# Attention values with v stationary in four column tiles, normalised once a sequence, and the turn loop written out

## The chip, the cores and the metric

The kernel runs on one NeuronCore of a Trainium2 chip. The metric is the device time of one launch in microseconds (us). Engine names: TensorE (PE; PEld is its weight loads), VectorE (DVE), ScalarE (ACT), GpSimd (POOL), SyncE (SP, which only issues transfers here).

## The reference

Two layers over 8 sequences of 512 tokens, 128 channels wide; in each layer an attention-like block and a feed-forward block read the same normalised input and are added to the residual.

```python
x = hidden                                   # (8, 512, 128)
xn = layernorm(x)
x = x + mamba(xn) + moe_top1(xn)             # layer 0: state space scan, 8 experts
xn = layernorm(x)
x = x + window_attention(xn) + glu_ffn(xn)   # layer 1

# window_attention: 16 heads of 8 channels, window of 32 tokens to either side
q, k, v = split_heads(x @ Wq + bq), split_heads(x @ Wk + bk), split_heads(x @ Wv + bv)
scores = einsum('bhqd,bhkd->bhqk', q, k) / sqrt(8) + mask      # |i - j| <= 32
probs = softmax(scores)
attn = einsum('bhqk,bhkd->bhqd', probs, v)
return merge_heads(attn) @ Wo + bo
```

## The kernel before

**Turns.** The 8 sequences go through a software pipeline. Turn `it` does the projections of layer 0 for sequence `it + 1` (lane "pre"), the scan for sequence `it` ("scan"), layer 1 for sequence `it - 1` ("attn") and the end of layer 1 for sequence `it - 2` ("finish"). Turns run from -1 to 9; turns -1 and 0 also carry the experts of layer 0. `iterations` writes turns -1, 0, 1 and 6 to 9 out and runs turns 2 to 5 as two passes of a hardware loop (`eng.Fori`) whose body holds two turns.

**Slots.** A turn has 28 slots. `plan()` lays out by hand what each slot holds, and every engine's program walks the same list (`units`) and issues its own part of each unit, in that order. So the order on each engine is fixed, and an engine that waits holds up all that is behind it. Of the 16 scan steps (n = 0 to 15) of a turn, four fall in every seven slots: VectorE scans 128x1024 values (`hst`, L711) and forms the next input (`dBu`, L703), ScalarE makes the decays (`dA`, L907), GpSimd multiplies by C (`hc`, L1072) and TensorE sums over the states in PSUM (`y_bank`, L1157).

**Attention.** The 512 queries of a sequence make 16 groups (g) of 32; a group sees 96 keys. The 16 heads lie as 4 ranges (r) of 4 heads, 32 channels a range. From slot 10 on, group g has its scores in slot 10 + g (L1230, L1232: a bank with 4 ranges of 96 keys for 4 x 32 rows of head and query), its row maxima in the same slot (`nmax`, L826), its four exponentials (`exp`, L989) and its four transposes (`turn`, L1238, copied out by ScalarE as `pT`, L994) in the next one. In every second slot the values of two groups are made (`values`, L1246): for each group and range `pT` (96 keys x 128 rows of head and query) is stationary and `vw` is streamed, 32 channels and a column of ones, three times over (`VREP`), so that each query gets a numerator for all 4 heads of the range and its denominator. VectorE then takes the reciprocal (`rden`, L837) and, in four multiplies of 32 rows each, picks the head's own 8 channels (`attn`, L841). Two banks take scores and transposes in turn; a third (`more`) takes the values and part of the feed-forward (`ffn` at slots 12, 16, 20: L1254, L997, L846, L850).

**End of layer 1.** In slot 0 of the next turn TensorE turns `attn` (L1258, L1260, 17 instructions), ScalarE adds `bv` (`attnT`, L1000), in slot 3 `fin` adds the feed-forward and the output projection (L1267, L1272, L1276), in slot 4 VectorE adds the residual (`y_out`, L854) and SyncE stores it (L552). In slots 0 to 3 also stand, for the next sequence, the gate (L806), the output projection (L1202), the residual (L810), the statistics with GpSimd's power for `rstd` (L1092) and the normalisation (L958).

**SyncE.** It issues the broadcast of each step's B and C rows (`bcr`, a ring of 4, L532), three of them in slot 27 before the turn, the others one by one, each after GpSimd's or VectorE's `hc` that frees the place; the loads `x_in` and `x_res` and the store of the output.

## Time and profile before

| | |
|---|---|
| median of 3 runs | 1193.38 us (1186.84 to 1199.42) |
| profiled execution | 1187.72 us, span 1185.9 us |
| mean granted TensorE clock | 0.932 of full speed |
| a turn with scan and attention, from gate to gate | 121.5 to 125.2 us |
| turn 8 (attention alone) and turn 9 | from 1098 us to the end |

The span is the time from the first to the last instruction of the profiled execution. A busy share of the whole span is a mean over stages of different kinds; the chain of work that ended last says at each moment which instruction the next one waited for.

### The profile page before, as it was taken

Reading aid. Unit: us, or ns where it says so; the run is one execution under the profiler, and the core shown is the slowest. Engines: PE = TensorE matmul, PEld = TensorE weight load, DVE = VectorE, ACT = ScalarE, POOL = GpSimd, SP = SyncE. Lnnn points to the kernel's source line nnn. Section 1 sums busy time; section 2 is a strip of 40 time slices with the busy share of each in tenths; the row PEclk is TensorE's granted clock in tenths of the full one; section 3 lists DMA queues with packets and bytes.
Section 4 is the critical chain, followed back from the end, with each engine's and each line's share of the span. In section 5 each row is a group of like instructions: output and inputs, shape, how many; then the busy total and the mean of one; then the engine's idle time right before and its main releaser. Section 6 shows DMA issues by size and latency. Waiting matters only on the chain.

```text
span 1185.9 us, 14605 instructions
## 1 busy us (share of the span) xinstructions
PE 915.9 (77%) x4474; PEld 580.8 (49%) x4474; DVE 851.5 (72%) x1301; ACT 614.4 (52%) x1410; POOL 410.6 (35%) x234
## 2 busy tenths in 40 slices
PE   4553788847887788778879787878787888788776
PEld 2422677723544454545546455545454545455555
DVE  7772543669779877888688868887879778777242
ACT  2142556635555655564556456555646563654542
POOL 2273222234632362237223632363225432532000
PEclk9666999988999999999999899989998998999998
DMA  8174888843312332233213331342234323530000
GB/s 275 54 208 128 234 246 288 235 108 87 90 57 77 76 87 73 74 80 89 74 56 95 84 91 54 89 89 81 62 70 96 80 54 77 110 80 10 9 1 10
DMA packets 79553, 116.78 MB, mean 98 GB/s; under 512 B 4848, under 2 KB 40048, under 8 KB 79344
## 3 DMA queue, kind: packets, MB, share of 16 engines
q1 hardware_dynamic: 73184, 108.99, 34.2%
q0 software_dynamic: 6288, 6.82, 2.6%
q8 instruction: 38, 0.62, 0.2%
q14 instruction: 43, 0.35, 0.1%
HBM read 103.73 MB, written 12.06 MB: 98 GB/s over the span
## 4 chain that ended last, share of the span: by engine, by line
PE 40%; DVE 22%; issue 14%; POOL 12%; ACT 9%; DMA 3%; DVEq 0%; POOLq 0%; SPq 0%; ACTq 0%
PE y_bank L1157 12%; DVE hst L711 9%; PE more L1246 6%; POOL hc L1072 6%; POOL xs_d L1040 3%; DVE dBu L703 3%; ACT pexp L989 3%; PE work_l L1238 3%; POOL x_res L1056 2%; ACT pT L994 2%; PE work_l L1232 2%; PE work L1238 2%; PE work L1272 1%; DMA hst<-in_hidden 1%; PE more L1254 1%
## 5 line engine op out<-in xcount | busy, mean ns | idle before, releaser
L1072 POOL TENSOR_TENSOR hc<-hst,bcr 128x1024 f32<-128x1024 f32 x116 | 280.0, 2414 | 606.5 <-DVE dBu L703 597.8
L1157 PE MATMUL y_bank<-hc,pk 128*128 128x512 f32 x512 | 270.6, 655 | 73.4 <-POOL hc L1072 62.8
L711 DVE TENSOR_TENSOR_SCAN hst<-dA,dBu 128x1024 f32<-128x1024 f32 x128 | 291.8, 2280 | 6.5 <-ACT dA L907 5.5
L1157 PEld LDWEIGHTS y_bank<-hc,pk 128*128 128x128 f32 x512 | 100.1, 207 | 187.7 <-POOL hc L1072 87.0
L907 ACT ACTIVATE dA<-dt,neg_a 128x511 f32<-128x511 f32 x256 | 171.6, 727 | 17.1 <-DVE hst L711 13.8
L703 DVE TENSOR_TENSOR dBu<-dtu,bcr 128x1024 f32<-128x1024 f32 x128 | 158.0, 1234 | 12.7
L1246 PE MATMUL more<-vw,pT 96*128 96x99 f32 x1024 | 129.2, 277 | 35.8 <-ACT pT L994 24.5
L1246 PEld LDWEIGHTS more<-vw,pT 96*128 96x128 f32 x1024 | 119.1, 191 | 68.3 <-DVE fsg L846 31.2
L994 ACT COPY pT<-work 96x512 f32<-96x512 f32 x64 | 37.3, 582 | 155.5 <-PE work L1238 155.5
L826 DVE TENSOR_REDUCE nmax<-work 128x4 f32<-128x384 f32 x64 | 35.5, 555 | 58.9 <-PE work L1232 58.9
L994 ACT COPY pT<-work_l 96x512 f32<-96x512 f32 x64 | 37.3, 582 | 62.2 <-PE work_l L1238 62.2
L989 ACT ACTIVATE pexp<-work_l,nmax 128x96 f32<-128x96 f32 x256 | 66.2, 342 | 5.9 <-DVE nmax L826 5.0
L989 ACT ACTIVATE pexp<-work,nmax 128x96 f32<-128x96 f32 x256 | 66.0, 344 | 6.0 <-DVE nmax L826 5.9
L841 DVE TENSOR_TENSOR attn<-more,rden 32x64 f32<-32x64 f32 x256 | 55.7, 218 | 8.2
L1056 POOL DMA_INDIRECT x_res<-ys_d,slot_b x32 | 51.3, 1604 | 9.3 <-issue 9.3
L1238 PEld LDWEIGHTS work_l<-pk,pexp 128*96 128x96 f32 x256 | 27.5, 126 | 50.2 <-ACT pexp L989 31.9
L1232 PE MATMUL work<-kT,qbd 128*128 128x384 f32 x128 | 51.7, 486 | 0.0
L1232 PE MATMUL work_l<-kT,qbd 128*128 128x384 f32 x128 | 51.6, 484 | 0.0
L1238 PEld LDWEIGHTS work<-pk,pexp 128*96 128x96 f32 x256 | 30.4, 129 | 41.5 <-issue 20.7
L1238 PE MATMUL work<-pk,pexp 128*96 128x128 f32 x256 | 40.5, 282 | 12.1 <-ACT pexp L989 12.1
L1238 PE MATMUL work_l<-pk,pexp 128*96 128x128 f32 x256 | 39.8, 277 | 12.4 <-ACT pexp L989 12.0
L738 DVE SCALAR_TENSOR_TENSOR z<-hs,half_c,z 128x512 f32<-128x512 f32 x48 | 48.0, 1051 | 0.0
(296 smaller groups left out, 1411.3 us busy)
## 6 DMA issues: line engine op xcount, KB each, us to landing
bcr<-bc_d SPq DMA_DIRECT2D x128, 512.0 KB, 5.0
qbd<-in_wx SPq DMA_DIRECT2D x8, 578.0 KB, 4.3
attn<-in_wx SPq DMA_DIRECT2D x8, 578.0 KB, 4.9
pT<-in_wx SPq DMA_DIRECT2D x8, 578.0 KB
kT<-in_wx SPq DMA_DIRECT2D x8, 578.0 KB, 5.0
vw<-in_wx SPq DMA_DIRECT2D x8, 578.0 KB, 4.9
xs_d<-rbuf POOLq DMA_DIRECT2D x1, 2560.0 KB, 9.8
hst<-in_hidden SPq DMA_DIRECT2D x8, 256.0 KB, 5.9
```

The costliest lines, as they stand in the source:

```text
L703: v.tensor_tensor(dBu[:], dtu[par], bcr[n % RING][:, 0:1, :].to_broadcast([P, NH, L]), ALU.mult).then_inc(s_dBu, 1)
L711: v.tensor_tensor_scan(hst[n % 2][:].rearrange("p h t -> p (h t)"), dA[n % 2][:].rearrange("p h t -> p (h t)"), dBu[:].rearrange("p h t -> ...
L841: last = v.tensor_tensor(attn[:, k - 1:k + 1, :, j, :], o[q, :, :, HD * j:HD * j + HD], rden[q, :, :].unsqueeze(3).to_broadcast([32, 2, RG ...
L907: s.activation(dA[n % 2][:, h, 1:L], dt[par][:, h, 1:L], ACT.Exp, scale=neg_a[:, h, n:n + 1]).then_inc(s_dA, 1)
L989: last = s.activation(pexp[k % 2][:, r, :], w1k(f"s{k}")[:, r * KW:(r + 1) * KW], ACT.Exp, bias=nmax[:, k, r:r + 1])
L994: s.copy(pT[k % 4][:], w1k(f"pT{k}")[0:KW, :]).then_inc(free1(f"pT{k}"), 1)
L1056: g_.indirect_dma_start(x_res[:, j, :], None, ys_d.rearrange("i j p d -> (i j p) d"), bass.IndirectOffsetOnAxis(ap=slot_b[:, j:j + 1], axi ...
L1072: g_.tensor_tensor(hc[n % 2][:], hst[n % 2][:], bcr[n % RING][:, 1:2, :].to_broadcast([P, NH, L]), ALU.mult).then_inc(s_hc, 1)
L1157: last = t.matmul(y_bank[h][:], ident, hc[n % 2][:, h, :], start=False, stop=(n == N - 1))
L1232: t.matmul(w1k(key)[:, 0:RG * KW], qbd[:, k, :, :].rearrange("p h q -> p (h q)"), kT[:, :, k * GQ:k * GQ + KW], start=False, stop=True).th ...
L1238: last = t.transpose(w1k(key)[0:KW, r * P:(r + 1) * P], pexp[k % 2][:, r, :], ident)
L1246: last = t.matmul(w1k(key)[:, a:a + VREP * 33].rearrange("p (n d) -> p n d", n=VREP), pT[(k - 1 + c) % 4][:, r * P:(r + 1) * P], vw[:, k - ...
```

## The change

- **Values.** `vw` is now stationary (96 keys x 32 channels) and `pT` streamed (96 x 128). Each of the four ranges writes its own 32 partitions of the bank, a column tile of the array. The bank then holds channels down and (head, query) across, 128 columns a group, for every pairing of a channel's head with a row's head. The ones and `VREP` are gone. ScalarE copies two groups at a time to `o_all`.
- **Denominators.** The exponentials write their row sums through `accum_out` into `den`, 64 of them a sequence. One reciprocal of 128x64 a sequence (`rden`, slot 27).
- **Own heads.** In slot 0 of the next turn SyncE issues 16 transfers inside SBUF, `o_all` to `o_own` (which is `fth`), 8 partitions each. TensorE turns `rden` (`rdT`), ScalarE copies it out, SyncE stores it to memory in 4 transfers, waits until they have landed, and loads it again with each row repeated to the 8 channels of its head (`rd_rows`, which is `y_out`).
- **Normalisation.** GpSimd multiplies the two (`avg`, slot 2, ahead of its part of `ln_a`), ScalarE adds `bv` (`attnT`, now slot 3, ahead of `ln_b`); VectorE's `averages` and TensorE's 17 instructions are gone. `fin` waits for `attnT` as before.
- **Loop.** `iterations` writes out all turns. The clearing of `vw` in turn 1 is gone.

```diff
-LAYER1_AT = {0: ["out"], 1: ["x1"], ... 6: ["v2", "v3"]}
-FINISH_AT = {2: ["attnT"], 3: ["fin"], 4: ["y_out"]}
-EDGE = [("attn", "y_end"), ("finish", "attnT"), ("pre", "xnT"), ("attn", "gated"), ("attn", "out")]
+LAYER1_AT = {0: ["out"], 1: ["x1"], ... 6: ["v2", "v3"], 27: ["rden"]}
+FINISH_AT = {0: ["rdT"], 2: ["avg"], 3: ["attnT", "fin"], 4: ["y_out"]}
+EDGE = [("attn", "y_end"), ("finish", "rdT"), ("pre", "xnT"), ("attn", "gated"), ("attn", "out")]
...
+        o_own = fth[:].rearrange("p (g q) -> p g q", q=GQ)
+        rd_rows = y_out[:].rearrange("p j d -> p (j d)")
...
         def iterations(eng, body):
-            body(-1, 1)
-            body(0, 0)
-            body(1, 1)
-            with eng.Fori(1, B // 2 - 1) as i:
-                body(i * 2, 0)
-                body(i * 2 + 1, 1)
-            for it in range(B - 2, B + 2):
+            for it in range(-1, B + 2):
                 body(it, it % 2)
...
# SyncE
+                    if name == "rdT":
+                        done1(sp, b, f"gate{HC - 1}")
+                        done1(sp, b, f"o{G // 2 - 1}")
+                        for r in range(RG):
+                            for h in range(4):
+                                q = slice(32 * r + HD * h, 32 * r + HD * h + HD)
+                                sp.dma_start(o_own[q, :, :], o_all[q, :, h, :]).then_inc(s_own, 16)
+                        done1(sp, b, "rdT")
+                        for r in range(RG):
+                            rows = rd_d[b, r] ...
+                            sp.dma_start(rows.rearrange("h g q -> g h q"), rdenT[r * G:(r + 1) * G, :, :]).then_inc(s_rdst, 16)
+                        sp.wait_ge(s_rdst, b * 64 + 64)
+                        before(sp, s_out, b * 16)
+                        sp.dma_start(rd_rows, ... .to_broadcast([RG * 4, HD, L])).then_inc(s_rdin, 16)
...
# VectorE
-                    v.memset(vw, 1.0).then_inc(s_clear, 1)
...
-                elif name == "averages":
-                    ...
-                    v.reciprocal(rden[:], o[:, :, :, 32]).then_inc(s_rden, 1)
-                    dve.wait_ge(s_rden, b * (G // 2) + k // 2 + 1)
-                    for j in range(4):
-                        q = slice(32 * j, 32 * j + 32)
-                        last = v.tensor_tensor(attn[:, k - 1:k + 1, :, j, :], o[q, :, :, HD * j:HD * j + HD],
-                                               rden[q, :, :].unsqueeze(3).to_broadcast([32, 2, RG, HD]), ALU.mult)
+                elif name == "rden":
+                    done1(dve, b, f"s{G - 1}")
+                    if not isinstance(b, int) or b >= 1:
+                        full1(dve, b - 1, "rdT")
+                    v.reciprocal(rden[:], den[:]).then_inc(s_rden, 1)
...
# ScalarE
                     for r in range(RG):
                         last = s.activation(pexp[k % 2][:, r, :], w1k(f"s{k}")[:, r * KW:(r + 1) * KW], ACT.Exp,
-                                            bias=nmax[:, k, r:r + 1])
+                                            bias=nmax[:, k, r:r + 1], accum_out=den[:, r, k:k + 1])
...
+                elif name == "averages":
+                    key = f"o{k // 2}"
+                    full1(act, b, key)
+                    if k == 1:
+                        before(act, s_own, b * 256)
+                    s.copy(o_all[:, k - 1:k + 1, :, :].rearrange("p g h q -> p (g h q)"),
+                           w1k(key)[:, 0:2 * P]).then_inc(free1(key), 1)
+                elif name == "rdT":
+                    full1(act, b, name)
+                    before(act, s_rdst, b * 64)
+                    s.copy(rdenT[:].rearrange("p h q -> p (h q)"), w1k(name)[0:RG * G, 0:P]).then_inc(free1(name), 1)
                 elif name == "attnT":
-                    full1(act, b, name)
-                    s.activation(attnT[:], w1k(name)[:], ACT.Identity, bias=pc("bv")).then_inc(free1(name), 1)
+                    act.wait_ge(s_avg, b + 1)
+                    done1(act, b, f"up{HC - 1}")
+                    s.activation(attnT[:], fth[:], ACT.Identity, bias=pc("bv")).then_inc(s_attnT, 1)
...
# GpSimd
+                    elif name == "avg":
+                        pool.wait_ge(s_own, b * 256 + 256)
+                        pool.wait_ge(s_rdin, b * 16 + 16)
+                        g_.tensor_tensor(fth[:], fth[:], rd_rows, ALU.mult).then_inc(s_avg, 1)
...
# TensorE
-                            a = (c * RG + r) * 33
-                            last = t.matmul(w1k(key)[:, a:a + VREP * 33].rearrange("p (n d) -> p n d", n=VREP),
-                                            pT[(k - 1 + c) % 4][:, r * P:(r + 1) * P],
-                                            vw[:, k - 1 + c, r, :].unsqueeze(1).to_broadcast([KW, VREP, 33]),
-                                            start=True, stop=True)
+                            last = t.matmul(w1k(key)[32 * r:32 * r + 32, c * P:(c + 1) * P], vw[:, k - 1 + c, r, :],
+                                            pT[(k - 1 + c) % 4][:, r * P:(r + 1) * P], start=True, stop=True)
...
-                elif name == "attnT":
+                elif name == "rdT":
                     take1_after(pe, b, name, f"o{G // 2 - 1}")
-                    t.matmul(w1k(name)[:, 0:2], identb[:], identb[:, 0:2], start=True, stop=True)
-                    for g in range(G):
-                        last = t.transpose(w1k(name)[:, g * GQ:(g + 1) * GQ],
-                                           attn[:, g, :, :, :].rearrange("p r h d -> p (r h d)"), ident[0:GQ, 0:GQ])
+                    pe.wait_ge(s_rden, b + 1)
+                    t.transpose(w1k(name)[0:RG * G, 0:P], rden[:].rearrange("p r g -> p (r g)"), ident).then_inc(s_full1, 1)
...
-                    done1(pe, b, "attnT")
+                    pe.wait_ge(s_attnT, b + 1)
```

## Rows read from the trace of the kernel before

**Rows 1.** The page, part 1: busy us (share of the span), instructions.

```profile
PE 915.9 (77%) x4474; PEld 580.8 (49%) x4474; DVE 851.5 (72%) x1301; ACT 614.4 (52%) x1410; POOL 410.6 (35%) x234
```

**Rows 2.** The chain that ended last, turn 4: start us, us, what.

```profile
683.82 2.03 PE more L1246 x16
...
689.84 1.03 ACT pexp L989 x4
...
697.95 0.21 DVE rden L837
...
709.15 1.04 ACT pexp L989 x4
...
723.10 2.04 PE more L1246 x16
...
742.11 0.21 DVE rden L837
```

**Rows 3.** The chain that ended last, turn 8: start us, us, what.

```profile
1158.53 2.00 PE more L1246 x16
...
1164.90 2.00 PE more L1246 x16
...
1171.26 2.01 PE more L1246 x16
```

**Rows 4.** Timeline of VectorE, turn 4 into 5: start us, us.

```profile
698.18 0.96 DVE L841 TENSOR_TENSOR attn<-more,rden 32x64 f32<-32x64 f32 x4
...
744.60 1.29 DVE L806 TENSOR_TENSOR dtu<-y_bank,sg 128x512 f32<-128x512 f32 x2
...
758.14 1.23 DVE L703 TENSOR_TENSOR dBu<-dtu,bcr 128x1024 f32<-128x1024 f32 x1
763.02 0.69 DVE L854 TENSOR_TENSOR y_out<-x1r,work 128x512 f32<-128x512 f32 x1 [3.64 <-PE work L1276]
```

**Rows 5.** Timeline of GpSimd, turn 5.

```profile
753.41 2.35 POOL L1072 TENSOR_TENSOR hc<-hst,bcr 128x1024 f32<-128x1024 f32 x1 [1.39 <-DVE dBu L703]
755.93 1.04 POOL L1092 TENSOR_TENSOR rstd<-var,minus_half 128x4 f32<-128x4 f32 x1 [0.17 <-DVE shift L823]
```

**Rows 6.** Timeline of TensorE, turn 5.

```profile
739.13 2.03 PE L1246 MATMUL more<-vw,pT 96*128 96x99 f32 x16 [0.67 <-ACT pT L994]
...
761.92 1.06 PE L1276 MATMUL work<-pk,fsg 128*128 128x128 f32 x8
```

**Rows 7.** The page, part 5, ScalarE: busy, mean ns of one, idle before.

```profile
L907 ACT ACTIVATE dA<-dt,neg_a 128x511 f32<-128x511 f32 x256 | 171.6, 727 | 17.1 <-DVE hst L711 13.8
...
L989 ACT ACTIVATE pexp<-work_l,nmax 128x96 f32<-128x96 f32 x256 | 66.2, 342 | 5.9 <-DVE nmax L826 5.0
```

**Rows 8.** Timeline of ScalarE, turn 5.

```profile
748.12 1.34 ACT L907 ACTIVATE dA<-dt,neg_a 128x511 f32<-128x511 f32 x2 [1.03 <-DVE hst L711]
...
759.90 1.65 ACT L958 ACTIVATE xn<-x1r,shift,rstd 128x128 f32<-128x128 f32 x4
```

**Rows 9.** SyncE's issues of bcr: duration ns min/median/max.

```profile
L532 SPq DMA_DIRECT2D bcr<-bc_d x128: 359/360/1984, 65.9 to 1064.8; - x128
```

**Rows 10.** DMA issues: KB each, median us to landing.

```profile
bcr<-bc_d SPq DMA_DIRECT2D x128, 512.0 KB, 5.0
...
out<-y_out SPq DMA_DIRECT2D x8, 256.0 KB, 2.4
```

**Rows 11.** Timeline of TensorE, the loop's back edge.

```profile
619.82 2.86 PE L1157 MATMUL y_bank<-hc,pk 128*128 128x512 f32 x4 [2.04 <-issue]
```

**Rows 12.** Timeline of VectorE, starts of turns 6 and 7.

```profile
866.06 1.29 DVE L806 TENSOR_TENSOR dtu<-y_bank,sg 128x512 f32<-128x512 f32 x2
...
988.94 1.29 DVE L806 TENSOR_TENSOR dtu<-y_bank,sg 128x512 f32<-128x512 f32 x2
```

**Rows 13.** Timeline of VectorE, the clearing in turn 1.

```profile
250.93 1.82 DVE L685 MEMSET vw<- 96x2112 f32 x1 [0.38 <-issue]
```

**Rows 14.** Windows, turn 4: PE, PEld, DVE, ACT, POOL busy (x), PEclk, DMA share, GB/s.

```profile
666.00:744.00 78.00, 66.03 (x313) 38.98 (x311) 61.36 (x97) 45.47 (x111) 29.73 (x16) 1.00 0.26 68
```

More of the change, by code:

```diff
@@ L58 @@
 CONSTS, FFN_CONSTS = 19, 21
-VREP = 3
 DVE_C = 4
@@ L72 @@
 PRE_AT = {0: ["xnT"], 1: ["hs0"], 2: ["hs1"], 3: ["zg0"], 4: ["conv1", "sg0"], 5: ["conv2", "zg1"], 6: ["conv3", "sg1"], 8: ["th1"], 9: ["xdbl"], 10: ["ss"], 12: ["xdr"], 13: ["bc"], 15: ["dtT"], 18: ["dtp0"], 19: ["drl0", "dtp1"], 21: ["drl1"], 22: ["de"], 23: ["dw"], 24: ["dln"], 25: ["dt"], 26: ["dtu"], 27: ["start"], 7: ["th0"]}
[L73 to L75 removed]
+LAYER1_AT = {0: ["out"], 1: ["x1"], 2: ["ln_a"], 3: ["ln_b"], 4: ["q", "k"], 5: ["v0", "v1"], 6: ["v2", "v3"], 27: ["rden"]}
+FINISH_AT = {0: ["rdT"], 2: ["avg"], 3: ["attnT", "fin"], 4: ["y_out"]}
+EDGE = [("attn", "y_end"), ("finish", "rdT"), ("pre", "xnT"), ("attn", "gated"), ("attn", "out")]
 LAG = {"pre": -1, "scan": 0, "attn": 1, "late": 2, "finish": 2}
@@ L171 @@
                  "ffn": [f"gate{_k}", f"up{_k}"], "ln_b": ["xnT"]}.get(
-                     _n, [_n] if _n in ("out", "q", "k", "v0", "v1", "v2", "v3", "attnT", "fin") else [])
+                     _n, [_n] if _n in ("out", "q", "k", "v0", "v1", "v2", "v3", "rdT", "fin") else [])
         L1_TURN += [(LAG[_lane], _key) for _key in _keys]
-L1_BANK = {"out": 0, "xnT": 1, "q": 0, "k": 1, "v0": 2, "v1": 0, "v2": 1, "v3": 2, "attnT": 2, "fin": 0,
+L1_BANK = {"out": 0, "xnT": 1, "q": 0, "k": 1, "v0": 2, "v1": 0, "v2": 1, "v3": 2, "rdT": 2, "fin": 0,
            **{f"s{k}": k % 2 for k in range(G)}, **{f"pT{k}": k % 2 for k in range(G)},
@@ L190, in l1_before, with program @@
     return b * (first + second) + (first + second) * lag - first - 2 * second + sum(i < at for q, i in uses)
-def program(nc, hidden, pack, wx_d, ffn_d, xn_d, xs_d, ys_d, bc_d, out):
+def program(nc, hidden, pack, wx_d, ffn_d, xn_d, xs_d, ys_d, bc_d, rd_d, out):
     ctx = ExitStack()
@@ L296, in program @@
         kT = sb("kT", [P, RG, L + 2 * WIN])
-        vw_all = sb("vw", [P, G, RG, HD * 4 + 1])
+        vw_all = sb("vw", [P, G, RG, HD * 4])
         vw = vw_all[0:KW]
@@ L302, in program @@
         pT = [pT_all[0:KW, k, :] for k in range(4)]
-        rden = sb("rden", [P, 2, RG])
-        attn_all = sb("attn", [P, G, RG, 4, HD])
-        attn = attn_all[0:GQ]
+        den = sb("den", [P, RG, G])
+        rden = sb("rden", [P, RG, G])
+        rdenT = sb("rdenT", [RG * G, 4, GQ])
+        o_all = sb("o_all", [P, G, 4, GQ])
         fth = sb("fth", [P, L])
@@ L324, in program @@
         q_flat = qbd[:].rearrange("p g h q -> p (g h q)")
-        a_flat = attn_all[:].rearrange("p g r h d -> p (g r h d)")
+        a_flat = o_all[:].rearrange("p g h q -> p (g h q)")
         p_flat = pT_all[:].rearrange("p k q -> p (k q)")
@@ L398, in program @@
         s_stat1, s_rstd1, s_xn1 = sem("stats1_ready"), sem("rstd1_ready"), sem("xn1_ready")
-        s_nmax, s_rden, s_attn, s_fth = sem("nmax_ready"), sem("rden_ready"), sem("attn_ready"), sem("ffn_tanh_ready")
+        s_nmax, s_rden, s_fth = sem("nmax_ready"), sem("rden_ready"), sem("ffn_tanh_ready")
+        s_own, s_rdst, s_rdin = sem("own_head_rows_in"), sem("rden_stored"), sem("rden_rows_in")
+        s_avg, s_attnT = sem("averages_ready"), sem("attnT_ready")
         block = ctx.enter_context(nc.Block())
@@ L549, in body @@
                         sp.dma_start(x_in[:], seq(xn_d, b + 1)).then_inc(s_xin, 16)
+                    if name == "rdT":
[7 more added lines that the diff above has]
+                        for r in range(RG):
+                            rows = rd_d[b, r] if isinstance(b, int) else rd_d[bass.ds(b, 1), r].rearrange("o h g q -> (o h) g q")
+                            sp.dma_start(rows.rearrange("h g q -> g h q"), rdenT[r * G:(r + 1) * G, :, :]).then_inc(s_rdst, 16)
+                        sp.wait_ge(s_rdst, b * 64 + 64)
+                        before(sp, s_out, b * 16)
+                        rows = rd_d[b:b + 1] if isinstance(b, int) else rd_d[bass.ds(b, 1)]
+                        sp.dma_start(rd_rows, rows.rearrange("o r h g q -> (o r h) (g q)").unsqueeze(1).to_broadcast(
+                            [RG * 4, HD, L])).then_inc(s_rdin, 16)
                     if name == "y_out":
@@ L979, in layer1 @@
                     full1(act, b, name)
-                    s.copy(vw[:, 4 * j:4 * j + 4, :, 0:32],
+                    s.copy(vw[:, 4 * j:4 * j + 4, :, :],
                            w1k(name)[0:KW, :].rearrange("p (g r d) -> p g r d", g=4, r=RG)).then_inc(free1(name), 1)
@@ L987, in layer1 @@
                         full1(act, b - 1, f"pT{G - 2 + k}")
+                    if k == 0:
+                        before(act, s_rden, b)
                     for r in range(RG):
                         last = s.activation(pexp[k % 2][:, r, :], w1k(f"s{k}")[:, r * KW:(r + 1) * KW], ACT.Exp,
-                                            bias=nmax[:, k, r:r + 1])
+                                            bias=nmax[:, k, r:r + 1], accum_out=den[:, r, k:k + 1])
                     last.then_inc(free1(f"s{k}"), 1)
@@ L1345 @@
     bc_d = nc.dram_tensor("bc_d", (B, 2 * N, L), F32, kind="Internal").ap()
-    program(nc, *args, xn_d, xs_d, ys_d, bc_d, out)
+    rd_d = nc.dram_tensor("rd_d", (B, RG, 4, G, GQ), F32, kind="Internal").ap()
+    program(nc, *args, xn_d, xs_d, ys_d, bc_d, rd_d, out)
     r = run_bass_kernel_spmd(nc, [arrays], core_ids=[0])
```

12 lines of the change are left out of this document (1 added, 11 removed).

## The prediction

> **What bounds the kernel now.** I read the page's busy times first: TensorE 77%, VectorE 72%, ScalarE 52%, GpSimd 35% of the span [rows 1]. No engine is full, so the question is who waits for whom, and I went to the chain that ended last, for one turn of the steady part (turn 4, 622 to 745 us) and for turn 8, which has attention and no scan. In turn 4 the chain changes engine at almost every unit. From slot 10 on a group goes scores, maxima, exponentials, transposes, copy, and back to scores or on to the values. In this chain the values stand 3 times, VectorE's reciprocal with its four multiplies 4 times, a block of four exponentials 3 times (the first at 689.84, the last at 709.15) [rows 2], where of each kind the first and the last are shown. In turn 8 a pair of groups takes 6.37 us from one values block to the next [rows 3]. In slots 0 to 4 VectorE has idle time of its own: 3.64 us before `y_out` [rows 4], and GpSimd follows with `rstd` right behind its product [rows 5]. So a removed piece counts if it is on this chain, and only until the next-late one takes over.
>
> **Values.** The block of 16 passes lasts 2.03 us [rows 6]. After the change there are again 16 passes, of 128 streamed columns. Such passes stand in `fin`: 8 in 1.06 us [rows 6], so with 0.28 us for the last, (1.06 - 0.28) / 7 = 0.11 us apart. One after another, 16 of them take 16 x 0.11 + 0.17 = 1.9 us: 0.1 us gained. If the four column tiles work side by side: 4 x 0.11 + 0.17 = 0.6 us, 1.4 us gained. No row shows column tiles. I take 1.0 us, since two passes of one tile follow each other with the weights changed between, but those of neighbouring tiles need not: 3 on the chain x 1.0 = 3.0 us a turn.
>
> The Trainium skill, page TensorEngine Tiling (Array Packing), section Key Properties, says that tiles are independent and can load weights and multiply in parallel, which would put the block at the 0.6 us end; it also says that a change of tiling mode drains the engine, which speaks against this change (a rival, below). No row here shows either.
>
> **Averages.** Reciprocal 0.21 us and four multiplies in 0.96 us, 1.2 us with the gaps [rows 2, 4]; 4 x 1.2 = 4.8 us, less one reciprocal of 64 columns in their place, estimated at 0.3 us: 4.5 us a turn. The other four blocks of a turn lie beside TensorE's work and give nothing directly.
>
> **Row sums.** This is the cost. I count a read of the sum behind each exponential as a further small instruction, because each goes to an own column of `den`. No row shows one. Bounds: nothing at all, if it is part of the exponential; at most a whole row of the present size, 0.34 us [rows 7]. Between them: a block of four takes 1.03 us [rows 2], so they follow each other at (1.03 - 0.34) / 3 = 0.23 us; two `dA` of 511 columns take 1.34 us and one 0.73 [rows 7, 8], so 0.61 us; the slope is (0.61 - 0.23) / 415 = 0.92 ns a column, and the part without columns 0.23 - 0.09 = 0.14 us in spacing and 0.34 - 0.09 = 0.25 us in duration. I take 0.2 us, 0.8 us a block. The blocks stand between maxima and transposes, so with the other two pieces shorter more of them reach the chain: going through turn 4 slot by slot I count 5 to 6 in place of 3. 5.5 x 0.8 = 4.4 us lost a turn. Beside other work, and so at nothing, I put ScalarE's copies to `o_all`, some 0.4 us a pair: it is idle 48% of the time [rows 1], and after them it waits for transposes anyway; without that cover they would cost 8 x 0.4 = 3.2 us a turn. TensorE's 17 turning instructions give nothing either, since behind them it waits for VectorE's gate.
>
> **What is late next.** Where a sum of y moves up it meets GpSimd's product of 2.35 us [rows 5], which starts only when VectorE has formed `dBu`; estimate 0.7 us a turn. `attnT` moves from slot 0, where ScalarE is idle, to slot 3 ahead of the normalisation `xn`: 0.6 us.
>
> **The queue of transfers.** SyncE issues 16 transfers, 4 stores, waits for these to land, then issues the load. An issue is 0.36 us [rows 9]; a transfer lands in 2.4 (store of the output) to 5.0 us (a 512 KB broadcast) [rows 10]. From the end of the last values: copy 0.4, 16 issues 5.8, 4 issues 1.4, landing 2.4, issue 0.4, landing 3.7 (between the two rows): 14.1 us. Queued behind on SyncE are `x_in` and the fourth `bcr`; on GpSimd behind `avg` stand `rstd` and the third product; on ScalarE behind `attnT` stands `xn`; on TensorE behind `fin` the queries and keys. In turn 5 the last values end at 739.13 + 2.03 - 1.0 = 740.1 us [rows 6], so the rows are in at 754.2. GpSimd is at its second product until 755.8 [rows 5], so it doesn't wait; the multiply of half that size, 1.2 us, pushes `rstd` from 755.9 to 757.0, and `xn` starts at 759.90 [rows 8], 2.7 us after `rstd` and its shift are through now: covered. `attnT` is ready before the last part of `fin` at 761.92 [rows 6]. The fourth `bcr` is issued at 754.2 - 3.7 + 0.7 = 751.2 and lands 5 us later at 756.2, before the `dBu` that reads it (758.14), behind which are another 3.64 us of idle time [rows 4]. So nothing a turn, with about 2.7 us of cover. At the end of the kernel nothing covers it. Now 1185.9 - 1173.3 = 12.6 us follow the last values [rows 3]; then 14.1 + `avg` 1.2 + `attnT` 0.7 + `fin` 1.0 + `y_out` 0.7 + issue and landing 2.8 = 20.5 us: 8 us lost once.
>
> **Loop and clearing.** TensorE stands 2.04 us at the back edge [rows 11]: 2.0 us gained once. Inside a turn I see nothing to gain: turn 5, in the loop, lasts 866.06 - 744.60 = 121.5 us, turn 6, written out, 988.94 - 866.06 = 122.9 us [rows 4, 12]. The cleared `vw` gives 1.82 + 0.38 = 2.2 us, on the chain [rows 13].
>
> **Sum.** A turn: 3.0 + 4.5 - 4.4 - 0.7 - 0.6 = 1.8 us, for the 7 turns with scan and attention 12.6 us. Turn 8: the pair's chain loses 1.0 us of values and 0.45 us of transposes that now stand before the maxima only because the averages do, and gains 0.8 us of sums: 0.65 x 8 = 5.2 us. Total 12.6 + 5.2 + 2.2 + 2.0 - 8.0 = 14.0 us less than the profiled execution's 1187.72, so 1173.7. That execution is 5.7 us below the median of the runs; for the median I forecast 1193.4 - 14.0 = 1179 us.
>
> **Rivals.** (1) The queue of transfers comes late; slower. Mechanism: GpSimd waits in slot 2, and `rstd`, `xn`, the queries and keys wait behind it. The rows speak for 0.36 us an issue, but all are of pieces of 512 B or more, and the 16 transfers carry 128 pieces of 128 B each and lie on 8 partitions. If an issue took 0.8 us, the queue would be 16 x 0.44 = 7 us longer; 2.7 us are covered, 4.3 lost in each of 7 turns, and 7 at the end: 30 + 7 = 37 us, 1216. It decides from 2.7 us on.
> The Trainium skill, page DMA: Bandwidth & Descriptors, section Specifications, wants 512 B a transfer for full rate and says that below it the engine reads, modifies and writes. It gives no time for 128 B, and no run here shows one; the sum above stays as it is.
> (2) A read costs a whole row, 0.34 us: 0.57 us more a block, 5.5 x 0.57 x 7 + 8 x 0.57 = 26 us: 1205.
> (3) The tiles don't work side by side (the change doesn't do what it says): 0.9 us more a block of values, 3 x 0.9 x 7 + 8 x 0.9 = 26 us: 1205.
> (4) Reads are nearly hidden (0.05 us): 0.6 x 5.5 x 7 + 8 x 0.6 = 28 us better: 1151.
> (5) Each change between tiled and untiled costs what a pass takes beyond its spacing, 0.28 - 0.11 = 0.17 us, twice a pair: 0.33 x 3 x 7 + 0.33 x 8 = 10 us: 1189. This is the drain that the page TensorEngine Tiling of the Trainium skill names.
>
> **How the numbers follow.** Chances: forecast 0.37, (1) 0.20, (2) 0.12, (3) 0.10, (4) 0.15, (5) 0.06. The runs of before spread by 1%, so I count a change within 1% (11.9 us: 1181.4 to 1205.3) as none. The forecast lies just beyond it and gives 0.22 to faster and 0.15 to same; (4) goes to faster; (5), half of (2) and (3) to same; (1) and the rest to slower; some of (2) and (3) may be met by cheaper terms elsewhere. That makes 0.41 faster, 0.31 same, 0.28 slower. With both best ends (1.4 us of values, no cost of sums) a turn would give 7.4 us, with both worst it would lose 4; the 80% range reaches to (4) and (1): 1148 to 1216.
>
> **What would show it.** The values: a block of 16 passes in about 1.0 us (0.6 and 1.9 for the ends). The sums: how long ScalarE needs from the first to the last instruction of a block of exponentials, 1.8 us against 1.03. VectorE's busy time down by about 8 x 8 x 1.2 = 77 us. GpSimd's wait before `avg`: none, or short, in rival (1) some microseconds in each turn. The end: 20 us from the last values to the end of the span. The prediction is wrong if the averages' place on the chain is taken in full by something I took for covered, the sums' blocks above all, or if TensorE, less busy, is granted its lower clock in the attention slots, where turn 4 now has the higher one throughout [rows 14].

## The result, and the profile after

The changed kernel takes 1207.57 us (median, 1206.69 to 1210.4) where the kernel before took 1192.95 us on the same chip: a ratio of 1.0113, interval 1.0080 to 1.0146. It is slower by 1.1%. The forecast was 1179 us and faster: the kernel moved the other way. The time lies inside the stated range of 1148 to 1216 us, on the side of rival (1).

The page of the changed kernel, parts 1 and 4 and groups of part 5 (line, engine, operation, out<-in; busy us, mean ns; idle before and what ended most of it):

```profile
span 1204.9 us, 13666 instructions
...
PE 846.3 (70%) x4346; PEld 489.3 (41%) x4346; DVE 795.1 (66%) x988; ACT 679.2 (56%) x1994; POOL 421.4 (35%) x242
...
PE 29%; issue 20%; POOL 15%; ACT 10%; DVE 10%; SPq 8%; DMA 6%; POOLq 0%; DVEq 0%; ACTq 0%
...
L1265 PE MATMUL more<-pT,vw 96*32 96x128 f32 x1024 | 41.2, 278 | 37.3 <-ACT pT L998 25.9
L1102 POOL TENSOR_TENSOR fth<-fth,y_out 128x512 f32<-128x512 f32 x8 | 10.1, 1262 | 146.3 <-DMA y_out<-rd_d 146.3
...
L993 ACT ACTIVATION_READ_ACCUMULATOR pexp<-work,nmax 128x1 f32 x256 | 52.9, 207 | 0.0
```

Against [rows 1], VectorE's busy time is down by 56 us and TensorE's by 70 us, and the kernel is slower. The two rows to see are the new ones without much work in them: GpSimd stands 146.3 us before its eight multiplies `avg`, each time for the load of `rd_d` (81.8 us of it before the last one, where it had no other work since the scans ended), and 8% of the span of the chain that ended last is SyncE issuing transfers (SPq), which computes nothing.

The queue in turn 5, from the timelines of SyncE, TensorE, GpSimd, VectorE and ScalarE of the changed kernel (start us, us; the bracket is the idle time before and what ended it):

```profile
740.57 11.65 SPq L554 DMA_DIRECT2D fth<-o_all  x16
752.27 1.86 SPq L558 DMA_DIRECT2D rd_d<-rdenT  x4
757.12 0.58 SPq L562 DMA_DIRECT2D y_out<-rd_d  x1
757.80 0.53 SPq L547 DMA_DIRECT2D x_in<-xn_d  x1
758.38 1.52 SPq L530 DMA_DIRECT2D bcr<-bc_d  x3
...
739.43 0.64 PE L1265 MATMUL more<-pT,vw 96*32 96x128 f32 x16 [0.76 <-ACT pT L998]
...
763.03 2.08 PE L1290 MATMUL work<-pk,fsg 128*128 128x128 f32 x8 [3.79 <-ACT fsg L1016]
...
760.97 1.26 POOL L1102 TENSOR_TENSOR fth<-fth,y_out 128x512 f32<-128x512 f32 x1 [8.04 <-DMA y_out<-rd_d]
762.19 1.04 POOL L1112 TENSOR_TENSOR rstd<-var,minus_half 128x4 f32<-128x4 f32 x1
...
764.29 1.23 DVE L716 TENSOR_TENSOR dBu<-dtu,bcr 128x1024 f32<-128x1024 f32 x1 [9.07 <-DMA bcr<-bc_d]
...
762.26 0.72 ACT L1016 ACTIVATE fsg<-fth,pk 128x512 f32<-128x512 f32 x1 [5.11 <-POOL fth L1102]
763.54 1.65 ACT L960 ACTIVATE xn<-x1r,shift,rstd 128x128 f32<-128x128 f32 x4 [0.56 <-POOL shift L1114]
```

The last values end at 740.07 us. The 16 issues take 11.65 us, 0.73 apiece with the gap; the rows are in at 760.97, 20.9 us after the values. Everything that was queued behind comes late: `rstd` behind `avg` on GpSimd, `xn` behind `attnT` on ScalarE (VectorE's gate is at 742.02 here, so `xn` starts 21.5 us after it; before it started 759.90 - 744.60 = 15.3 us after it [rows 4, 8]), and the three `bcr` behind `x_in` on SyncE. And `fin` takes 2.08 us where it took 1.06 [rows 6]: after its idle stretch TensorE's granted clock is lower (the windows further below show 0.76 of full speed in 756 to 768 us and 1.00 in the 14 us ahead of them).

Where the 19.0 us of span went (1185.9 to 1204.9), from each turn's gate, first scores (the first `bandb` matmul after it) and the start of its last block of values on the timelines of both kernels; turns 2 to 6 as means:

| stretch | before | after |
|---|---|---|
| turns 2 to 6: gate to first scores | 42.7 | 47.1 |
| turns 2 to 6: first scores to last values | 74.9 | 73.8 |
| turns 2 to 6: last values to next gate | 5.3 | 2.6 |
| turn 7: the same three | 33.9, 70.7, 3.8 | 40.0, 65.7, 2.6 |
| turn 8: gate to scores, scores to last values, to the end | 18.5, 55.5, 14.6 | 31.8, 49.8, 27.1 |

From first scores to the next gate the change gains: 5 x 3.8 + 6.2 in turn 7 + 5.7 in turn 8 + 4.2 in turn 1 = 35.1 us. From the gate to the scores and at the end it loses: 5 x 4.4 + 6.2 + 13.3 + 12.5 at the end, less 1.1 in turn 1 = 52.9 us; the first gate comes 1.5 us later. Net 19.3, beside 19.0 measured.

The profiled execution of the kernel before is one of its shortest (1187.7 us, median 1193.0), and that of the changed kernel lies at its median, so that the spans differ by 19.0 us and the medians by 14.6. The rows of one execution hold such a spread too: in e6 below, the kernel before with its loop written out, the end takes 17.3 us and turn 8 from gate to scores 19.9, for 14.6 and 18.5 in the table.

The end, in the chain that ended last of the changed kernel (start us, us, what):

```profile
1177.77 0.68 PE more L1265 x16
...
1178.47 0.38 ACT o_all L1007
...
1179.67 0.70 SPq L554
...
1190.07 0.69 SPq L554
...
1192.23 1.47 DMA rd_d<-rdenT
1193.71 3.36 DMA y_out<-rd_d
...
1199.28 2.09 PE work L1290 x8
...
1201.46 0.69 DVE y_out L856
```

Of the 16 issues, 15 stand on the chain itself, one behind another from 1179.67 to 1190.76: 11.1 us in which it waits for SyncE alone. The first runs beside TensorE's and ScalarE's work on `rden`.

### The profile page after: what moved, and what is told of

Its sections match the earlier page's. It is cut to its first block, busy times and chain, and to the rows that moved or that the text cites. A ratio compares the mean times of both kernels' runs of the same rounds, so it can differ in the third digit from the quotient of the medians.

```text
span 1204.9 us, 13666 instructions
## 1 busy us (share of the span) xinstructions
PE 846.3 (70%) x4346; PEld 489.3 (41%) x4346; DVE 795.1 (66%) x988; ACT 679.2 (56%) x1994; POOL 421.4 (35%) x242
## 4 chain that ended last, share of the span: by engine, by line
PE 29%; issue 20%; POOL 15%; ACT 10%; DVE 10%; SPq 8%; DMA 6%; POOLq 0%; DVEq 0%; ACTq 0%
PE y_bank L1177 10%; POOL hc L1088 7%; SPq L554 7%; POOL x_res L1072 4%; ACT pexp L993 3%; POOL xs_d L1056 3%; DVE hst L724 3%; DMA y_out<-rd_d 2%; PE work_l L1258 2%; ACT pT L998 2%; PE work L1258 2%; PE work L1196 2%; DMA hst<-in_hidden 1%; DMA rd_d<-rdenT 1%; DVE dBu L716 1%
## 5 line engine op out<-in xcount | busy, mean ns | idle before, releaser
L716 DVE TENSOR_TENSOR dBu<-dtu,bcr 128x1024 f32<-128x1024 f32 x128 | 165.3, 1291 | 58.6 <-DMA bcr<-bc_d 46.7
L993 ACT ACTIVATE pexp<-work,nmax 128x96 f32<-128x96 f32 x256 | 83.3, 340 | 5.0 <-DVE nmax L839 4.9
L993 ACT ACTIVATE pexp<-work_l,nmax 128x96 f32<-128x96 f32 x256 | 83.3, 338 | 3.0 <-DVE nmax L839 3.0
L839 DVE TENSOR_REDUCE nmax<-work_l 128x4 f32<-128x384 f32 x64 | 35.5, 554 | 51.0 <-PE work_l L1252 51.0
L1265 PE MATMUL more<-pT,vw 96*32 96x128 f32 x1024 | 41.2, 278 | 37.3 <-ACT pT L998 25.9
L1102 POOL TENSOR_TENSOR fth<-fth,y_out 128x512 f32<-128x512 f32 x8 | 10.1, 1262 | 146.3 <-DMA y_out<-rd_d 146.3
L751 DVE SCALAR_TENSOR_TENSOR z<-hs,half_c,z 128x512 f32<-128x512 f32 x48 | 56.6, 1229 | 0.0
L1265 PEld LDWEIGHTS more<-pT,vw 96*32 96x32 f32 x1024 | 25.0, 109 | 69.5 <-issue 38.3
L993 ACT ACTIVATION_READ_ACCUMULATOR pexp<-work,nmax 128x1 f32 x256 | 52.9, 207 | 0.0
```

The source lines that it names most:

```text
L716: v.tensor_tensor(dBu[:], dtu[par], bcr[n % RING][:, 0:1, :].to_broadcast([P, NH, L]), ALU.mult).then_inc(s_dBu, 1)
L839: v.tensor_reduce(nmax[:, k, :], w1k(f"s{k}")[:, 0:RG * KW].rearrange("p (r k) -> p r k", r=RG), AX_X, ALU.max, negate=True).then_inc(s_nm ...
L993: last = s.activation(pexp[k % 2][:, r, :], w1k(f"s{k}")[:, r * KW:(r + 1) * KW], ACT.Exp, bias=nmax[:, k, r:r + 1], accum_out=den[:, r, k ...
L1265: last = t.matmul(w1k(key)[32 * r:32 * r + 32, c * P:(c + 1) * P], vw[:, k - 1 + c, r, :], pT[(k - 1 + c) % 4][:, r * P:(r + 1) * P], star ...
```

## The experiments

The theory that I tested (A): the time to issue the 16 transfers, nearly twice what the rows of before showed, puts the normalisation and what is queued behind it late. The main rival (B): the row sums on ScalarE take the gain back. A further question (A2) was which wait of A decides, that of `avg` or that of `bcr`.

**e1, without the 16 transfers.** The waits for them go too.

```diff
-                        for r in range(RG):
-                            for h in range(4):
-                                sp.dma_start(o_own[q, :, :], o_all[q, :, h, :]).then_inc(s_own, 16)
-                        pool.wait_ge(s_own, b * 256 + 256)
```

> The changed kernel without the 16 transfers that pick the own heads (fth keeps what the feed-forward left; the output is not the reference's). Theory A, the queue of transfers: 16 issues of 0.73 us are 11.7 us of a queue that takes 20.4 us from the last values to the rows of rden, and this is what made the stretch from the gate to the first scores 4 to 7 us longer a turn, 13 us in turn 8, and the end 12.5 us. It expects the queue at 8.7 us, the stretch back at about 42 us in turns 2 to 6 and 20 us in turn 8, the end 11.7 us shorter: 50 to 60 us less than the changed kernel, about 1150 us. Rival B, the reads of the sums on ScalarE took the gain: it expects only the end to be shorter, about 1196 us.

Measured: 1158.08 us, ratio to before 0.9719 (0.9695 to 0.9744). Gate to scores falls to between 41.3 and 41.7 us in turns 2 to 6, to 23.5 in turn 8, and the end to 17.1. GpSimd in turn 5 of e1, timeline:

```profile
733.84 2.35 POOL L1084 TENSOR_TENSOR hc<-hst,bcr 128x1024 f32<-128x1024 f32 x1 [1.32 <-DVE dBu L712]
736.15 1.27 POOL L1097 TENSOR_TENSOR fth<-fth,y_out 128x512 f32<-128x512 f32 x1
```

`avg` follows the product without a wait, as the prediction had it for 0.36 us an issue. And `fin` of turn 5, with no idle stretch ahead of it, takes 1.06 us again:

```profile
742.34 1.06 PE L1285 MATMUL work<-pk,fsg 128*128 128x128 f32 x8
```

The span is 51.0 us shorter than that of the changed kernel: 5.4 us a turn in the mean of turns 2 to 6, 5.7 in turn 7, 8.2 in turn 8, 10.0 at the end. Theory A holds, and its size is well over the whole loss; B could at most explain what is left beside it.

**e2, the fourth `bcr` before the turns.** All four places of the ring are filled at the start, so that each later load is issued one slot sooner, ahead of the 16 transfers.

```diff
-                        for n in range(RING - 1):
+                        for n in range(RING):
-                    if name == "spread" and k + RING - 1 < N:
+                    if name == "spread" and 0 < k and k + RING - 1 < N:
```

> The changed kernel with the fourth bcr issued with the first three, ahead of the 16 transfers. Both are theory A, and they differ in who behind the queue decides. A1, the fourth bcr decides (VectorE waits 9.1 us for it in turn 5, 46.7 us in all): that wait goes and the kernel gets some 40 us shorter, about 1168 us. A2, the normalisation decides (GpSimd's avg, behind it rstd, ScalarE's attnT and xn, TensorE's fin, VectorE's y_out): the wait for bcr goes and comes back as one for fin, less than 8 us gained, 1200 to 1208 us. Rival B expects no change.

Measured: 1201.01 us, ratio 1.0061 (1.0034 to 1.0088). The waits of VectorE in the changed kernel (us in total, times, longest):

```profile
DVE dBu L716 <- DMA bcr<-bc_d: 46.7, 6, 9.1
...
DVE y_out L856 <- PE work L1290: 40.1, 3, 24.6
```

and the waits of e2:

```profile
POOL fth L1102 <- DMA y_out<-rd_d: 148.8, 8, 83.2
...
DVE y_out L856 <- PE work L1290: 84.7, 8, 24.8
```

VectorE's wait for `bcr`, 46.7 us in six times in the changed kernel, is gone, and a wait of the same engine for `fin` has grown from 40.1 to 84.7 us in its place. So the long idle before `dBu` was the wait that the profile shows, not the one that decides: behind it stood the normalisation. Only 6.6 of the 50 us come back, and the intervals of the two ratios just touch.

**e3, without the row sums.** `den` is filled with 8 once, and the exponentials write no sums.

```diff
-                                            bias=nmax[:, k, r:r + 1], accum_out=den[:, r, k:k + 1])
+                                            bias=nmax[:, k, r:r + 1])
```

> The changed kernel without the row sums: no accum_out, den is set once to 8 (the output is not normalised rightly). A block of exponentials is then 1.03 us in place of 1.40. Theory A: 0.37 us a block, 5.5 blocks a turn on the chain, in 7 turns, and 8 in turn 8: 17 us, about 1191 us, all of it between the first scores and the last values. Rival B, the sums took the gain of the change: 30 us or more, 1178 us or less.

Measured: 1195.43 us, ratio 1.0041 (1.0019 to 1.0062), 12 us less than the changed kernel by the medians and 9 by the ratios. ScalarE's timeline, a block of four exponentials in e3:

```profile
689.69 1.03 ACT L994 ACTIVATE pexp<-work,nmax 128x96 f32<-128x96 f32 x4
```

and such a block in the changed kernel:

```profile
689.95 0.35 ACT L993 ACTIVATE pexp<-work_l,nmax 128x96 f32<-128x96 f32 x1
690.19 0.20 ACT L993 ACTIVATION_READ_ACCUMULATOR pexp<-work_l,nmax 128x1 f32 x1
690.28 0.34 ACT L993 ACTIVATE pexp<-work_l,nmax 128x96 f32<-128x96 f32 x1
...
691.13 0.21 ACT L993 ACTIVATION_READ_ACCUMULATOR pexp<-work_l,nmax 128x1 f32 x1
```

The read is an instruction of its own, with a row of 0.2 us, but most of that lies under the next exponential: from the start of the first to the end of the last read 1.39 us pass instead of 1.03, so a read costs 0.09 us. Rival B's mechanism is there, but at 12 us in all beside the 50 of e1. (From first scores to the next gate e3 is 15 us shorter; some of it is lost again ahead of the scores.)

**e4, values without column tiles.** All 128 channels of `vw` are stationary, so each pass covers the whole array. The passes of the four ranges write the same 128 columns one after another, and only the last range's values stay.

```diff
-                            last = t.matmul(w1k(key)[32 * r:32 * r + 32, c * P:(c + 1) * P], vw[:, k - 1 + c, r, :],
+                            last = t.matmul(w1k(key)[:, c * P:(c + 1) * P],
+                                            vw[:, k - 1 + c, :, :].rearrange("p r d -> p (r d)"),
```

> The changed kernel with the values' 16 passes on the whole array: 128 channels stationary, the four ranges write the same 128 columns one after another (only the last range's are right). Prices the column tiles: the block goes from 0.64 us to about 1.9 us. If the values are on the chain 3 times a turn as in the chain of before: 3 x 1.3 x 7 + 8 x 1.3 = 38 us more, 1245 us. If other work has taken their place there: under 15 us more, below 1222 us.

Measured: 1244.73 us, ratio 1.0458 (1.0424 to 1.0492), 37 us more than the changed kernel. TensorE's timeline of e4:

```profile
702.11 2.05 PE L1265 MATMUL more<-pT,vw 96*128 96x128 f32 x16 [0.47 <-DVE fsg L848]
```

The same 16 passes take 0.64 us with column tiles. The four tiles do work side by side, and the change does what it says: 1.4 us a block, 3 x 1.4 x 7 + 8 x 1.4 = 40.6 us by the prediction's way of counting, beside 37 measured. The sum fits better than its parts: turns 2 to 6 are 2.7 us longer each in the mean where this count has 4.2, turn 7 is 9.2 us longer, turn 8 up to its last values 9.1 where it has 11.2, and the end 3.1.

**e5, the own heads picked on GpSimd.** In place of the 16 transfers GpSimd multiplies `o_all` by a mask of 128 channels x 4 heads and adds the four parts up: three instructions for groups 0 to 13 in slot 27, three for the last two in slot 0. It computes the whole reference.

```diff
+            def pick(b, part):
+                g, ng = ((0, G - 2), (G - 2, 2))[part]
...
+                g_.tensor_tensor(o, o, pc("heads").unsqueeze(1).unsqueeze(3).to_broadcast([P, ng, RG, GQ]), ALU.mult)
+                g_.tensor_tensor(o[:, :, 0:2, :], o[:, :, 0:2, :], o[:, :, 2:4, :], ALU.add)
+                g_.tensor_tensor(o_own[:, g:g + ng, :], o[:, :, 0, :], o[:, :, 1, :], ALU.add)
```

> A version that computes the reference: the changed kernel with the own heads picked on GpSimd (o_all times a mask of heads, two adds; 14 of the 16 groups in slot 27, the last two in slot 0) in place of the 16 transfers. Theory A: the queue is as short as without the transfers (e1_no_own, 1158 us); GpSimd has some 14 us between its last product of a turn and the first of the next, and the mask work is about 8 us of it: 1156 to 1166 us. If GpSimd's work slows VectorE beside it or delays the first product, 1170 us or more.

Measured: 1169.48 us (1165.64 to 1170.93), ratio to before 0.9808 (0.9773 to 0.9844): 1.9% below the kernel before and some 3% below the changed one. It keeps 38 of the 50 us that e1 gave. The other 10 us of span (1163.9 against 1153.9) lie in turns 2 to 6, 120.6 us long in the mean against 118.0: 12.8 us in all, of which other stretches give some back. From last values to the gate these turns take 3.8 to 4.4 us, e1 2.6: 7.8 us of the 12.8. GpSimd and VectorE there, timelines of e5:

```profile
721.69 3.24 POOL L1091 TENSOR_TENSOR o_all<-o_all,pk 128x1792 f32<-128x1792 f32 x1 [2.65 <-ACT o_all L1001]
725.00 2.95 POOL L1094 TENSOR_TENSOR o_all<-o_all 128x896 f32<-128x896 f32 x1
728.03 1.99 POOL L1096 TENSOR_TENSOR fth<-o_all 128x448 f32<-128x448 f32 x1
...
721.30 2.28 DVE L718 TENSOR_TENSOR_SCAN hst<-dA,dBu 128x1024 f32<-128x1024 f32 x1
723.62 2.39 DVE L733 TENSOR_TENSOR hc<-hst,bcr 128x1024 f32<-128x1024 f32 x1
725.93 3.10 DVE L805 TENSOR_TENSOR dtu<-dt,u 128x1024 f32<-128x1024 f32 x1
...
729.42 1.69 DVE L710 TENSOR_TENSOR dBu<-dtu,bcr 128x1024 f32<-128x1024 f32 x1
```

VectorE's operation of 128x1024 with two inputs takes 1.23 us elsewhere [rows 4]; here 2.39 and 3.10. The starts and ends take turns: GpSimd ends at 724.93 and VectorE's `hc` 1.1 us later, GpSimd's next ends at 727.95 and `dtu` 1.1 us after that. Each seems to stand until the other's instruction is through. The Trainium skill, page SBUF — State Buffer, section Who interferes with whom, says that a VectorE instruction with two inputs in SBUF contends with a GpSimd instruction that reads SBUF, and calls the ports that they share an exclusive lock. These rows agree, in time, not only in sum. The scan in the first row of VectorE reads one of its inputs, `dBu`, from PSUM, and keeps its usual 2.28 us beside GpSimd's multiply.

**e6, only the loop of before written out.**

```diff
-            with eng.Fori(1, B // 2 - 1) as i:
-                body(i * 2, 0)
-                body(i * 2 + 1, 1)
-            for it in range(B - 2, B + 2):
+            for it in range(-1, B + 2):
```

> The kernel before with the loop written out and nothing else. The traces show 2 us of TensorE's idle time at the back edge, and turns of equal length in and out of the loop: 1 to 3 us less than before, within what can be told. Rival: the loop's register work costs in every turn, 6 us or more less.

Measured: 1194.05 us, ratio 1.0015 (0.9994 to 1.0035): no change. The back edge's idle time is gone from TensorE's timeline. The turn that held it gets shorter, 122.9 us from gate to gate for 125.2, but the two behind it get longer, 122.9 each for 121.9 and 121.5.

**e7, the stores of `rdenT` ahead of the 16 transfers**, so that their landing is hidden under the issues (the four stores and their wait for `rdT` moved up, nothing else).

> The changed kernel with the 4 stores of rden ahead of the 16 transfers, so that their landing (1.5 to 3.4 us) lies under the transfers' issues. Theory A: the queue is shorter by the landing, but starts when rden is turned, about 2 us after the last values; 0 to 3 us less in each of 8 uses: 1190 to 1207 us. If the landing was covered anyway, no change.

Measured: 1204.52 us, ratio 1.0092 (1.0057 to 1.0128), 3 us less than the changed kernel, with intervals that overlap. In turn 5 the load is issued 15.94 us after the end of the last values (in the changed kernel 17.05). The landing is hidden, but the stores' wait for `rdT` now stands ahead of the 16 issues, and these still take 11.66 us, so 1.1 us come back.

**e8, four wide transfers** in place of the 16: again 2048 pieces of 128 B a sequence, but 32 partitions and 512 pieces a transfer instead of 8 and 128.

```diff
-                            for h in range(4):
-                                q = slice(32 * r + HD * h, 32 * r + HD * h + HD)
-                                sp.dma_start(o_own[q, :, :], o_all[q, :, h, :]).then_inc(s_own, 16)
+                            q = slice(32 * r, 32 * r + 32)
+                            sp.dma_start(o_own[q, :, :], o_all[q, :, 0, :]).then_inc(s_own, 16)
```

> The changed kernel with 4 transfers of 32 partitions (512 pieces of 128 B each) in place of 16 of 8 partitions (128 pieces each); they take the first of the four heads everywhere, so the output is not the reference's. Tells what an issue depends on. A1, the number of transfers: 4 x 0.73 us, the queue at 11.6 us, close to e1_no_own, 1158 to 1166 us. A2, the number of pieces: as long as the 16, 1200 to 1208 us, with issues of 2.8 us.

Measured: 1158.32 us, ratio 0.9713 (0.9673 to 0.9754), as fast as without any transfer. SyncE's issues, durations in ns (min/median/max), of e8:

```profile
L553 SPq DMA_DIRECT2D fth<-o_all x32: 596/629/845, 368.2 to 1139.1; - x32
```

and of the changed kernel, with the other two kinds of its queue:

```profile
L554 SPq DMA_DIRECT2D fth<-o_all x128: 685/686/912, 369.3 to 1190.1; - x128
...
L558 SPq DMA_DIRECT2D rd_d<-rdenT x32: 425/426/453, 381.3 to 1192.2; - x32
...
L562 SPq DMA_DIRECT2D y_out<-rd_d x8: 575/582/626, 384.2 to 1193.7; - x8
```

Four times the pieces in one transfer cost no more to issue (0.63 against 0.69 us). So for these shapes the price is by the transfer, and the bytes and pieces themselves, moved in e8 just the same, cost nothing that shows. The four issues that are left lie under other work in the turns; at the end, where nothing covers them, e8 takes 18.7 us and e1 17.1.

**e9 to e11, two edits to e5**: the early `bcr` of e2 (e9), GpSimd's first pick cut in two at slots 22 and 27 (e10), both (e11).

```diff
-                g, ng = ((0, G - 2), (G - 2, 2))[part]
+                g, ng = ((0, 8), (8, G - 10), (G - 2, 2))[part]
...
-                    if name == "rden":
+                    if (name, k) == ("averages", 9):
                         pick(b, 0)
+                    if name == "rden":
+                        pick(b, 1)
```

> The heads are picked on GpSimd as in e5_mask_pool, and all four bcr loads of the first turn's ring are issued before the turns, so that from then on a bcr load is issued one slot sooner, as in e2_early_bcr. Theory A, that after the 16 transfers are gone SyncE's queue is late for nobody: in e5 no wait of VectorE on bcr is left among the large ones, so nothing changes: 1166 to 1173 us. Theory B, that the bcr loads behind the store and load of rdenT still hold the scans by a little each turn: 8 x 0.5 to 1 us back, 1161 to 1165 us.

> As e5_mask_pool, but the first pick is cut in two: groups 0 to 7 at slot 22, groups 8 to 13 at slot 27, the last two as before, so 9 operations in place of 6 and the same elements. Theory C: in e5 the first pick's 8.2 us on GpSimd run beside VectorE's hc, dtu and dBu at the turn's end, which take 2.4, 3.1 and 1.7 us where 1.2 to 1.4 were usual, some 4 us in all, and the turn from the last values to the next gate is 4.4 us long where e1_no_own had 2.6. With 3.5 us of it at the turn's end the stretch falls to about 3.3 us, and what VectorE loses at slot 22 costs nothing or as much again: 1160 to 1169 us, and the stretch from last values to gate shows it. Theory D, that e5's 11 us over e1_no_own have nothing to do with the place of the picks: 1168 to 1172 us, the stretch unchanged at 4.4 us.

> Both edits, of e9_mask_bcr and e10_mask_spread. If they act on different waits their gains add up: with theories A and C 1160 to 1169 us, with B and C 1154 to 1163 us, with A and D 1168 to 1172 us.

Measured: e9 1169.42 us, ratio 0.9789 (0.9724 to 0.9855); e10 1167.66 us, 0.9784 (0.9719 to 0.9849); e11 1165.38 us, 0.9765 (0.9696 to 0.9833). e9 is e5 again: the waits of e5 and of e9 have none of VectorE for a `bcr` load, so that none is late once the 16 transfers are gone. e10 shortens the stretch from last values to gate to 3.1 us in turns 4 to 6, as theory C said, but in turns 2 and 3 it is 3.8 and 4.35, and gate to scores is some 2 us longer in turns 3 and 4 than in e5; 1.8 us of median can't be told from nothing. e11 has the lowest time of the versions that compute everything, 4 us under e5, with intervals that overlap. What the picks cost beside VectorE is shown; that it makes up all of the 10 us is not.

## Why the prediction was wrong

**The step that failed is "The queue of transfers".** It priced an issue at 0.36 us, from the `bcr` row [rows 9], and took a queue of 14.1 us from the last values. It lasts 20.9 us in turn 5:

| part | predicted | measured |
|---|---|---|
| copy and first issue | 0.4 | 0.5 |
| 16 issues | 5.8 | 11.7 |
| 4 stores issued, landed | 3.8 | 4.9 |
| issue and landing of the load | 4.1 | 3.8 |

Of the 6.8 us beyond, 5.9 lie in the 16 issues and 1.1 in the stores. Against a cover of 2.7 us, 4.1 should show in a turn. The stretch from gate to scores grew by 4.4 in turns 2 to 6, but e1, which is 1.2 us shorter there than the kernel before, says that the transfers cost 5.4 a turn. So the queue was let off 1.3 us too much a turn; TensorE's lower clock after the wait, `fin` at 2.08 us in turn 5 for 1.06 in e1, is 1.0 of it.

Rival (1) had the mechanism, the place and nearly the issue's price (0.8 against 0.73). Its 37 us came out as 51 (e1): 5.4 to 5.7 us in each of turns 2 to 7 in place of 4.3, 8.2 in turn 8, which has no scan beside which the queue could hide, and 10.0 in place of 7 at the end. Turn 8 loses 13.3 us from gate to scores in all; the other 5.0 stay in e1 (23.5 against 18.5), where GpSimd still waits for the store and load. That the time lies inside the range is partly luck: the queue was dearer than in rival (1), whose 1216 us is the range's upper end, and the rest of the kernel better than forecast.

The fault in reasoning is in the choice between the bounds. 0.36 us was the minimum and the median of the one kind of transfer looked at, a broadcast of 512 KB; the transfers of the change differ from it in partitions, pieces and where they read. The text named that difference and gave it 0.20, but took the sum at the low end with no row for it. With 16 in one chain, 0.17 us an issue was all the cover allowed for.

**Also wrong in the same step**: the fourth `bcr` lands not at 756.2 but at 764.3, after the wait of 9.07 us that VectorE shows; e2 shows that this was not the one that decides.

**Values**: 1.0 us gained was predicted, 1.4 measured (2.03 to 0.64), the end of the range with the tiles side by side; rival (3) is refuted by e4. Rival (5), a drain at each change of tiling, has no time left to stand in: the whole block with both changes of mode around it lasts 0.64 us, as for 16 passes of four tiles without it, and the matmul behind it starts at 740.00, before its end at 740.07.

**Averages**: not measured by themselves. VectorE's busy time fell by 56 us, not 77: the two groups gone were 55.7 + 13.1 us in part 5 of the page of before, the new reciprocals take 4.4, and two groups that stayed became longer, `dBu` from 158.0 to 165.3 us and the `z` chain of 128x512 from 48.0 to 56.6. GpSimd's work moved beside them: in turn 5 two of the `z` take 3.13 us from 766.03 on, beside GpSimd's product from 765.60 to 767.95, where the same two took 1.41 us in the kernel before. Whether that is the cause wasn't tried here (e5 shows what it can do). What the averages brought in time is worked out under "Late next" as far as it can be.

**Row sums**: mis-sized as well, and the other way: 0.2 us a read predicted, 0.09 measured, and 12 us in all where 4.4 x 7 + 6.4 = 37 were put down. Rival (2) falls; rival (4), 0.05 us a read, was near. A bound from a row's duration said little about its cost in a row of instructions that overlap.

**Late next, loop, clearing**: from first scores to the next gate 35 us were gained where the terms of this stretch come to 24: 29 for values, 35 for averages (with the transposes of turn 8), 2 for the loop, less 37 for sums and 5 for what is late next. That is no proof of the terms. In the same stretches e4 is 35 us longer than the changed kernel and e3 15 us shorter. If these two prices add up, values and sums make 20 of the 35 us, and 15 are left for averages, late next and loop together, where 32 were put down. So these three came out some 17 us short of the forecast. The loop's 2 are part of that; how the rest falls on averages and late next no run shows. The clearing's 2.2 us fall from gate to scores in turn 1, where 1.1 were gained. The loop's 2.0 us were not gained: e6 shows 1.0015. The prediction had the hint in [rows 4, 12], turns in the loop shorter than those written out, and counted the idle time at the back edge all the same.

**The end**: 20.5 us from the end of the last values were predicted, 26.5 measured (1204.9 - 1178.4): 6.1 more in the 16 issues (1178.92 to 1190.8) and 1.2 in `fin` at the lower clock, less 1.5 in the stores and the load.

**Clock**: I feared the lower clock in the attention slots. In those of turn 4 the granted clock is 0.96 where it was 1.00 [rows 14]; what that costs was not measured. In turn 8 TensorE has the full clock in them, and the lower one around the waits. Windows of the changed kernel (from:to, us, busy of PE, PEld, DVE, ACT and POOL, PEclk, DMA share, GB/s):

```profile
666.00:744.00 78.00, 59.24 (x311) 28.59 (x311) 57.13 (x61) 54.41 (x186) 30.29 (x16) 0.96 0.29 70
...
742.00:756.00 14.00, 9.61 (x37) 4.97 (x36) 12.84 (x19) 5.99 (x11) 4.69 (x2) 1.00 0.17 23
756.00:768.00 12.00, 8.21 (x41) 6.53 (x40) 3.71 (x3) 4.40 (x9) 4.81 (x4) 0.76 0.69 196
...
1100.00:1125.00 25.00, 12.36 (x57) 9.45 (x57) 2.62 (x13) 7.21 (x13) 2.46 (x3) 0.66 0.13 29
1125.00:1178.00 53.00, 36.05 (x262) 19.34 (x265) 13.60 (x23) 37.36 (x160) 0.00 (x0) 1.00 0.00 1
1178.00:1205.00 27.00, 7.19 (x50) 6.30 (x41) 0.69 (x1) 1.35 (x3) 1.26 (x1) 0.64 0.15 31
```

In sum: with the forecast's own terms the span would have been 14.0 us shorter; what lies between gate and scores and at the end came out 41 us worse (53 lost where 12 were put down, by the queue and the lower clock), the attention 9 us better, and the start 1.5 us later. That is +19, by the two profiled executions.

## What to carry to other kernels

Price the issue of a transfer by a row of its own kind, and where there is none, count what the chain bears before choosing: so many issues times the doubt in one. Many small transfers in a row on one queue are serial work like any other, with the wait and everything queued behind them on every engine; fewer and wider ones moved the same number of pieces for nothing that showed here, and six instructions on GpSimd did the same job for some 10 us. A long wait named by the profile is the last to end, not always the one that decides: take it away alone before building on it.
